# Values of the first attention: four of eight key tiles as three fp16 products

## The reference

```python
q = (v @ WQ).reshape(B, S, H, C)          # 16 batches, S = 1024, H = 8 heads, C = 64
k = (v @ WK).reshape(B, S, H, C)
val = (v @ WV).reshape(B, S, H, C)
scores = jnp.einsum('bshc,bthc->bsth', q, k) * SCALE
A = jax.nn.softmax(scores, axis=2)
u = jnp.einsum('bsth,bthc->bshc', A, val).reshape(B, S, H * C)
return u @ Wout + bout
```

## Time and profile before

| | us |
|---|---|
| median of 3 runs | 4938.34 (4937.33 to 4940.33) |
| the profiled execution | 4936.12 |
| its span | 4934.4 |
| TensorE busy in the span | 4631.5 (94%) |
| VectorE | 3639.3 (74%) |
| ScalarE | 3153.1 (64%) |
| GpSimd | 2212.3 (45%) |

### The profile page before, as it was taken

One profiled execution on the slowest core, in us unless ns is written; L12 is line 12 of the kernel. 1 busy time (PEld: TensorE's weight loads), 2 busy tenths in 40 slices (PEclk: granted clock), 3 DMA queues, 4 the chain that ended last, 5 costly groups with the idle time before them and its releaser, 6 DMA issues. The chain is left out here.

```text
span 4934.4 us, 105574 instructions
## 1 busy us (share of the span) xinstructions
PE 4631.5 (94%) x42323; PEld 2051.7 (42%) x42323; DVE 3639.3 (74%) x6356; ACT 3153.1 (64%) x3450; POOL 2212.3 (45%) x2149
## 2 busy tenths in 40 slices
PE   5999979999999999999999979999999999999965
PEld 3434423333333333333333334444444444444433
DVE  4666756666666666666666668888888888888878
ACT  2433426666666666666666638888888888888844
POOL 2233243333323232333333346666666666666656
PEclk9999989999999999999999979999999999999966
DMA  4211100000000000000000000000000000000001
GB/s 102 69 52 52 52 1 1 1 1 1 1 1 1 1 1 1 1 1 1 1 1 1 1 1 3 2 2 2 2 2 2 2 2 2 2 2 2 2 7 28
DMA packets 43620, 51.39 MB, mean 10 GB/s; under 512 B 33416, under 2 KB 33544, under 8 KB 43144
## 3 DMA queue, kind: packets, MB, share of 16 engines
q1 hardware_dynamic: 40440, 44.03, 3.3%
q10 hardware_dynamic: 2704, 0.72, 0.1%
HBM read 39.73 MB, written 4.19 MB: 9 GB/s over the span
## 5 line engine op out<-in xcount | busy, mean ns | idle before, releaser
L1686 DVE TENSOR_REDUCE a_mp<-psum 128x1 f32<-128x512 f32 x2072 | 1323.6, 685 | 668.1 <-PE psum L1563 654.4
L2412 DVE TENSOR_REDUCE f_mp<-psum 128x1 f32<-128x512 f32 (+2 forms) x2352 | 1471.5, 682 | 187.3 <-PE psum L2234 171.1
L1531 ACT ACTIVATE a_prob<-psum,escale 128x1024 f32<-128x1024 f32 x1024 | 1087.0, 1111 | 523.9 <-PE psum L1612 523.9
L2194 ACT ACTIVATE f_prob<-psum,escale_f 128x1024 f32<-128x1024 f32 x1152 | 1248.2, 1113 | 215.8 <-PE psum L2311 108.0
L1620 PE MATMUL psum<-a_prob,a_v 128*64 128x512 f32 x4104 | 993.7, 605 | 0.0
L2234 PE MATMUL psum<-f_kf,f_qf 64*128 64x512 f16 (+2 forms) x3658 | 651.6, 307 | 41.2 <-DVE f_mp L2412 32.1
L2048 POOL TENSOR_SCALAR f_hi<-f_raw,part 128x512 f16<-128x512 f32 x324 | 507.2, 1565 | 392.9 <-ACT f_raw L2152 386.6
L1451 POOL TENSOR_TENSOR a_u<-a_og,a_inv 128x512 f32<-128x512 f32 x129 | 134.5, 1042 | 1166.4 <-DVE a_inv L1701 1166.4
L2324 PE MATMUL psum<-f_prob,f_vh 128*32 128x512 f32 (+3 forms) x6144 | 614.7, 495 | 9.1 <-DVE f_oc L2434 7.3
L2303 PE MATMUL psum<-f_qf,f_kf 64*128 64x512 f16 (+3 forms) x3074 | 505.1, 327 | 18.6 <-ACT f_og L2157 18.2
L1620 PEld LDWEIGHTS psum<-a_prob,a_v 128*64 128x64 f32 x4104 | 248.8, 136 | 504.6 <-issue 501.0
(11 more groups left out here) (440 smaller groups left out, 6729.5 us busy)
## 6 DMA issues: line engine op xcount, KB each, us to landing
idx<-in_itok_BS_dram SPq DMA_DIRECT2D x36, 512.0 KB, 6.0
idx<-in_itok_BS_dram SPq DMA_DIRECT2D x54, 256.0 KB, 6.9
idx<-in_x_dram SPq DMA_DIRECT2D x18, 256.0 KB, 3.6
a_qh<-a_rowT SPq DMA_DIRECT2D x258, 1.0 KB
out_dram<-h SPq DMA_DIRECT2D x16, 256.0 KB, 2.6
f_qf<-f_rowT SPq DMA_DIRECT2D x130, 4.0 KB, 1.7
wd<-in_L_ffn_Wd_dram SPq DMA_DIRECT2D x2, 256.0 KB
bd<-in_L_ffn_bd_dram ACTq DMA_DIRECT2D x16, 2.0 KB
```

Of the source, the lines that this page charges most:

```text
L1531: act.activation(prob[:, part], k.psum[:, pair:pair + 2].rearrange("p b n -> p (b n)"), ACT.Exp, scale=k.escale[:]).then_inc(s.read, 1)
L1686: dve.tensor_reduce(mp[:, tg % 2, t + 4 * r, c:c + 1], bank_of(j + r), X, ALU.max)\
L2194: act.activation(prob[:, u % NPF], k.psum[:, pair:pair + 2], ACT.Exp, scale=k.escale_f[:])\
L2412: dve.tensor_reduce(side[:, at[0]:at[-1] + 1:step], bank_of(j + r)[:, 0:len(at) * width].rearrange("p (a b) -> p a b", b=width), X, ALU.ma ...
```

## The change

Key tiles 0, 1, 4 and 5 are multiplied by the values in three fp16 products instead of one fp32 product: low values x high exponentials, high values x low ones, high x high. For that the exponentials and the values are split into parts. Tiles 0 and 4 are split by GpSimd (`halve`: a cast, then a subtraction of 128x1024). Tiles 1 and 5 get their high part from a ScalarE copy, issued after the exponential of the following tile (2 or 6), and their low part from VectorE (`low`, in slots 3 and 7, after that slot's reductions). The exponential gets a bias of 6 ln 2, which the division by the sum takes out again. GpSimd also splits the values once a batch (`twice`, behind head 6's `add`).

The order is moved: the pairs are now (0,1), (2,3), (6,7), (4,5), in slots 4, 6, and 1 and 2 of the next head. (0,1) and (4,5) are the fp16 pairs. "out" moves from behind slot 3 to behind slot 5, the copy to `un` from behind tile 1 to behind tile 3, the inverse from slot 6 to slot 7. GpSimd's order in a head becomes: `halve` of tile 0, `split_q`, in head 4 `prepare_batch`, in head 5 `split_x`, `halve` of tile 4, `add`, in head 3 `squares`, in head 6 `twice`. Five more memsets are done before the stage's start. Four semaphores of an earlier stage are used again.

```diff
-A_PARTS = ((0, 1), (2, 3), (4, 5), (6, 7))
+A_PARTS = ((0, 1), (2, 3), (6, 7), (4, 5))
+A_PART_OF = {kt: p for p, part in enumerate(A_PARTS) for kt in part}
+A_HALVED = {0: 0, 1: 1, 4: 2, 5: 3}
+A_LEVEL = 6 * math.log(2.0)
-A_VALUES_AT = (2, 4, 6, 9)
+A_VALUES_AT = (4, 6, 9, 10)
-A_EXTRA = {0: (('x', 0),), 1: (('q', 2),), 3: (('out', -1),)}
-A_COPY_AT = 1
-A_INVERSE_AT = 6
+A_EXTRA = {0: (('x', 0),), 1: (('q', 2),), 5: (('out', -1),)}
+A_COPY_AT = 3
+A_INVERSE_AT = 7
...
+                def twice(b, par, n):
+                    here = v[:, par, :, 0]
+                    pool.tensor_copy(vh[:, par], here).then_inc(s.p, 1)
+                    passed(pool, k.seen, s.p, n + 5)
+                    pool.tensor_tensor(vl[:, par], here, vh[:, par], ALU.subtract).then_inc(s.p, 1)
+                def halve(G, kt, count):
+                    at = A_HALVED[kt]
+                    passed(pool, k.seen, s.read, count)
+                    pool.tensor_copy(ph[:, at], prob[:, kt]).then_inc(s.p_high, 1)
+                    passed(pool, k.seen, s.p_high, n_half(G, kt))
+                    pool.tensor_tensor(pl[:, at], prob[:, kt], ph[:, at], ALU.subtract).then_inc(s.p_low, 1)
...
+                pool.memset(ph[:], 0.0).then_inc(s.clear, 1)
+                pool.memset(pl[:], 0.0).then_inc(s.clear, 1)
+                pool.memset(vh[:, 1], 0.0).then_inc(s.clear, 1)
+                pool.memset(vl[:, 1], 0.0).then_inc(s.clear, 1)
+                pool.memset(level[:], A_LEVEL).then_inc(s.clear, 1)
...
+                        b = i * 2 + x // HEADS + 1
+                        halve(G, 0, n_stream(i, x, "exp", 0))
+                        split_q(G + 2, (x + 2) % 4, n_stream(i, x, "q", 0))
+                        if x % HEADS == 4:
+                            prepare_batch(b, (x // HEADS + 1) % 2, b * 6)
+                        if x % HEADS == 5:
+                            split_x(b, (x // HEADS + 1) % 2, n_stream(i, x, "x", 0))
+                        halve(G, 4, n_stream(i, x, "exp", 4))
+                        add(i * 2 + (x - 1) // HEADS, (x + 1) % 2, G + 1)
                         if x % HEADS == 3:
                             squares(i * 2 + x // HEADS)
+                        if x % HEADS == 6:
+                            twice(b, (x // HEADS + 1) % 2, b * 6)
...
                             act.activation(prob[:, part], k.psum[:, pair:pair + 2].rearrange("p b n -> p (b n)"),
-                                           ACT.Exp, scale=k.escale[:]).then_inc(s.read, 1)
+                                           ACT.Exp, scale=k.escale[:], bias=level[:]).then_inc(s.read, 1)
+                            if part in (2, 6):
+                                act.wait_ge(s.read, n_stream(i, x, "exp", part - 1))
+                                act.activation(ph[:, A_HALVED[part - 1]], prob[:, part - 1], ACT.Copy).then_inc(s.p_high_act, 1)
...
+                    if A_PARTS[p][0] in A_HALVED:
+                        pe.wait_ge(s.p_low, n_half(G, A_PARTS[p][0]))
+                        pe.wait_ge(s.p_low_dve, n_half(G, A_PARTS[p][1]))
+                        for kt in A_PARTS[p]:
+                            at = A_HALVED[kt]
+                            for a, b in ((vl, ph), (vh, pl), (vh, ph)):
+                                for half in range(2):
+                                    last = pe.matmul(ps[A_SUM][halves(half)], lhsT=a[:, bp, kt],
+                                                     rhs=b[:, at, half * HALF:(half + 1) * HALF],
+                                                     start=(kt == first and a is vl), stop=(kt == final and a is vh and b is ph),
+                                                     skip_group_check=True)
+                        last.then_inc(s.pv, 1)
+                        return
...
+                def low(G, kt):
+                    at = A_HALVED[kt]
+                    dve.wait_ge(s.p_high_act, n_half(G, kt))
+                    dve.tensor_tensor(pl[:, at], prob[:, kt], ph[:, at], ALU.subtract).then_inc(s.p_low_dve, 1)
...
                             for j, kind, of, part in ROUNDS[x][u]:
                                 read_out(i, x, j, kind, of, part)
+                            if u in (3, 7):
+                                low(i * AROUND + x, u - 2)
```

More of the change, by code:

```diff
@@ L1 @@
 from contextlib import ExitStack
+import math
 import numpy as np
@@ L702, in layer0 @@
         E = {name: k.sem("l0_" + name) for name in L_EVENTS}
+        k.spent, k.spent_at = [E[name] for name in ("gT", "eg", "wT", "gturn")], PAIRS_
         def first(pair):
@@ L1315, in attention1 @@
         prob = sb("a1_prob", [P, NPB, S], F32)
+        ph = sb("a1_ph", [P, 4, S], FP16)
+        pl = sb("a1_pl", [P, 4, S], FP16)
+        vh = sb("a1_vh", [P, 2, T, C], FP16)
+        vl = sb("a1_vl", [P, 2, T, C], FP16)
+        level = sb("a1_level", [P, 1], F32)
         un = sb("a1_un", [P, HALF], F32)
@@ L1336, in attention1 @@
         s.q_split = k.sem("a1_q_split")
+        s.p_high, s.p_high_act, s.p_low, s.p_low_dve = k.spent
         s.inverse = k.sem("a1_inverse")
@@ L1364, in n_pv, with n_half @@
             return NAV * (G + 1) + p + 1
+        def n_half(G, kt):
+            return k.spent_at + 2 * (G + 1) + kt // 4 + 1
         def bank_of(j):
@@ L1469, in _ @@
                 pool.memset(v[:, 1], 0.0).then_inc(s.clear, 1)
+                pool.memset(ph[:], 0.0).then_inc(s.clear, 1)
[3 more added lines that the diff above has]
+                pool.memset(level[:], A_LEVEL).then_inc(s.clear, 1)
                 pool.sem_inc(s.summed, 1)
                 pool.sem_inc(s.scaled, 2)
-                pool.wait_ge(s.clear, 6)
+                pool.sem_inc(s.p_high, 2)
+                pool.sem_inc(s.p_low, 2)
+                pool.wait_ge(s.clear, 11)
                 prepare_batch(0, 0, 0)
+                twice(0, 0, 0)
                 split_x(0, 0, 1)
@@ L1515, in copy_out @@
                     act.activation(un[:], ps[A_SUM], ACT.Copy).then_inc(s.copied, 1)
+                act.sem_inc(s.p_high_act, 2)
                 for n, (kind, of, part) in enumerate(A_START_STREAM):
@@ L1519, in _ @@
                     read_out(0, -1, kind, of + 1, 2 * (n % 2))
-                act.wait_ge(s.clear, 6)
+                act.wait_ge(s.clear, 11)
                 for i in range(NB // 2):
@@ L1529, in _ @@
                                 continue
-                            act.wait_ge(s.pv, n_pv(G - 1, part // 2))
+                            act.wait_ge(s.pv, n_pv(G - 1, A_PART_OF[part]))
                             act.activation(prob[:, part], k.psum[:, pair:pair + 2].rearrange("p b n -> p (b n)"),
-                                           ACT.Exp, scale=k.escale[:]).then_inc(s.read, 1)
+                                           ACT.Exp, scale=k.escale[:], bias=level[:]).then_inc(s.read, 1)
+                            if part in (2, 6):
+                                act.wait_ge(s.read, n_stream(i, x, "exp", part - 1))
+                                act.activation(ph[:, A_HALVED[part - 1]], prob[:, part - 1], ACT.Copy).then_inc(s.p_high_act, 1)
                             if part == A_COPY_AT:
@@ L1613, in score, with values @@
                     return last
-                def values(x, p):
+                def values(G, x, p):
                     bp = (x // HEADS) % 2
+                    first, final = A_PARTS[0][0], A_PARTS[-1][-1]
+                    if A_PARTS[p][0] in A_HALVED:
[11 more added lines that the diff above has]
+                        return
                     for kt in A_PARTS[p]:
@@ L1621, in values @@
                                              rhs=prob[:, kt, half * HALF:(half + 1) * HALF],
-                                             start=(kt == 0), stop=(kt == T - 1), skip_group_check=True)
+                                             start=(kt == first), stop=(kt == final), skip_group_check=True)
                     last.then_inc(s.pv, 1)
@@ L1629, in _ @@
                 last.then_inc(s.pv, NAV - sum(at >= T for at in A_VALUES_AT))
-                pe.wait_ge(s.clear, 6)
+                pe.wait_ge(s.clear, 11)
                 for n, (kind, of, part) in enumerate(A_START_STREAM):
@@ L1654, in _ @@
                                             pe.wait_ge(s.read, n_stream(i, x, "exp", A_PARTS[p][-1]))
-                                            values(x, p)
+                                            values(G, x, p)
                                         if at == u + T:
                                             pe.wait_ge(s.read, n_stream(i, x - 1, "exp", A_PARTS[p][-1]))
-                                            values(x - 1, p)
+                                            values(G - 1, x - 1, p)
                                 else:
@@ L1669, in _ @@
                         pe.wait_ge(s.read, SS + SR * (NB // 2))
-                        values(-1, p)
+                        values(NB * HEADS - 1, -1, p)
```

(1 more changed line is left out.)

## The result

The changed kernel takes 5524.7 us (5522.7 to 5530.4), the kernel before 4938.2 in the same set of runs: 1.119 times as long (95% interval 1.1173 to 1.1206), +586 us where 462 were forecast. The direction and the place were right; the time lies 35 us above the top of the range.

What follows compares the result with a forecast made beforehand. TensorE, the bound before, would wait on equal loops through VectorE and GpSimd: 157.2 us a batch against 132.8, x16 = +390; clock 64, start 6, end 2 make +462, 5400 us on the median. Range 5190 to 5490.

Steps and rivals of the forecast that it cites:

- The saving of TensorE: In the values matmuls, two of four pairs becoming fp16 save 0.48 us each, 0.95 a head.
- the reading of "out": Before tile 7's score matmul, TensorE waits 0.21 us a head until "out" has been read.
- the start: Before the stage, GpSimd's extra clearing of buffers takes 4 to 9 us, taken as 6, all exposed.
- rival (e): `low` is ready before the first fp16 values matmul, so TensorE stays the bound: 4824 us; chance 3%.
- VectorE's loop: The first fp16 values matmul waits for `low`, queued behind VectorE's reductions: 17.85 us a head undisturbed.
- GpSimd's loop: `add` waits for the inverses; `halve` and `split_q` follow, and slot 4's maxima wait for that split: 17.8 us a head.
- The blocking: `low` waits out GpSimd's q subtraction because two-input VectorE instructions contend with it: 18.55 us a head instead of 17.8.
- 3.3 us for that head: In head 5, `low` asks in the middle of `split_x`'s 2.13 us subtraction, delaying the first fp16 values matmul by 3.3.
- the clock: In heads 4 and 7, long TensorE idling halves the clock, 2 us lost each: +64 us, bounds 0 and 200.
- my 6.30: TensorE's way from the first fp16 values matmul of a head to slot 7's maxima: 6.3 us.
- the end: After the last head, a second values matmul and its parts add 2 us.
- Rival (d): GpSimd's cast of tile 4 gets ahead of `low`, values matmul at 19.6 us: up to 5500; chance 9%.

Runs made afterwards that it cites:

- the two kernels without parts: Changed kernel with no exponential parts made and no waits for them: 4954.2 us; the same with all four pairs in fp32: 5057.5 us.
- opening them singly: Changed kernel with GpSimd's `add` behind the next head's `split_q`: 5426.0 us; separately, with tile 1's copy and `low` made earlier (slot 1): 5477.0 us.
- together: Changed kernel with both edits, `add` behind the next head's `split_q` and tile 1's copy and `low` made earlier: 4956.6 us.
- with it taken away: Changed kernel with VectorE's two-input subtraction in `low` replaced by a one-input reduction of the same tile: 5425.8 us.
- the fillers: Changed kernel with extra matmuls of constants into the free sum bank where TensorE waits: 5315.4 us.
- the kernel with the order mended: Against the all-fp32 kernel without parts in the moved order (5057.5 us): maxima before V(4,5) in slot 2, before the score tile in slot 6: 4964.8 us.

## Why the prediction was right in kind and wrong in size

- The saving of TensorE, 0.95 a head: measured 0.81 (the two kernels without parts). Nearly right, and 119 us of moved order and start, of which the prediction had 33 (27 for the reading of "out", 6 for the start), undo it. In the changed kernel the waits at the banks lie under the longer waits for `split_q` and `low` (1.59 and 0.78 in head 6), so this didn't spoil the sum. It did spoil rival (e): even with every part ready in time the kernel would have been 16 us slower than before, not 114 faster.
- VectorE's loop and GpSimd's loop, equally long: right, shown by opening them singly (99 and 48 us) and together (568). `low` cost 1.22 (I took 1.25).
- The blocking: right; 99 us with it taken away, 0.75 x 128 = 96 by the prediction. In head 5 it went the other way round. VectorE's `low` was issued just ahead of GpSimd's subtraction:
```profile
2210.69 1.22 DVE L1765 TENSOR_TENSOR a_pl<-a_prob,a_ph 128x1024 f16<-128x1024 f32 x1
2210.71 3.19 POOL L1469 TENSOR_TENSOR a_xl<-a_xraw,a_xh 128x1024 f16<-128x1024 f32 x1 [0.18 <-POOL a_xh L1467]
```
  so GpSimd was blocked (3.19 for 2.13) and TensorE hardly. I had 3.3 us for that head and it is 1.3 (V(0,1) from 2188.63 to 2212.05 is 23.4 us; less 18.5 and 3.7 of clock): 32 us less in all.
- **The step that failed is the clock**: the prediction lets it fall only in heads 4 and 7 ("2 us lost: x2 heads x16 = +64", with bounds of 0 and 200). That it falls and costs time on the path was right; the term was mis-sized. It measured 209. The same windows as the earlier trace rows, for the plain head 6 above:
```profile
2062.00:2064.00 2.00, 1.22 (x10) 0.70 (x12) 2.00 (x3) 0.15 (x1) 1.89 (x1) 0.95 0.00 0
2064.00:2066.00 2.00, 2.00 (x14) 0.81 (x9) 0.40 (x2) 0.00 (x0) 1.93 (x1) 0.50 0.01 4
2066.00:2068.00 2.00, 2.00 (x24) 1.52 (x20) 1.29 (x2) 0.45 (x1) 0.19 (x1) 0.69 0.01 1
```
  Before the fall TensorE had idled 1.59 us, done one M and idled 0.78; the clock fell to 1.2 GHz when it was already at work on V again. I had taken the one row with an unbroken idle of 5.50 as the kind of wait that matters. Seven of eight heads fall (only head 5, with 0.33 and 1.64 idle, doesn't in the batch I read). From V(0,1) to M(7), my 6.30, it is 6.34 in head 5 and 7.91 in head 6 (2063.14 to 2071.05), and 10.0 in head 4: (6 x 1.6 + 3.7) x 16 = 213, beside the 209 of the fillers. Head 7 takes 10.3 instead of 7.8 in about every second batch; over all 128 heads this way is 224 us longer than 128 x 6.34.
- The start: M and V begin 9.6 us later (734.6 and 744.2), I had 6; the end, +2, is within 1.

In sum: 390 + 64 + 8 was forecast. Of the 586, 209 are the clock, some 10 the start, and the 367 that are left the loops, with the blocking and the savings in them. So the miss of 124 is 145 of clock and 4 of start too little, and some 25 of loops and end too much, where head 5's 32 lie.

Rival (d) is given as "up to 5500", but its own V at 19.6 makes 1.05 x 128 = 134 more, 5534. That this is near the measured 5525 is chance: in (d) GpSimd's cast of tile 4 gets ahead of `low`, and the rows of head 6 show `low` ahead of the cast.

## What to carry to other kernels

Before moving work to engines with room, draw the loop: which instruction of theirs starts after what of the bound engine, what is queued ahead of it, and where the bound engine stands until it is done. Two loops of the same length hide each other: removing either one gave 99 and 48 us, removing both gave 568, the clock's loss included, since either loop alone kept TensorE waiting enough to lower the clock (0.93 and 0.92 over the run). When a full TensorE begins to wait in each round, price its clock in each round, not only behind the longest waits.

## What the runs showed of the hardware that I had not expected

- The clock can fall to 1.2 GHz after two waits of 1.6 and 0.8 us with a pair of matmuls between them (0.50 in the window 2064 to 2066), and matmuls of constants in these waits kept it at 1.00 in the loop.
- An exponential of 128x1024 from PSUM with a scale and a bias per partition took 1.204 us in the mean, with the scale alone 1.111. The Trainium skill (ScalarE: Activation LUTs, What ACT_TABLE_LOAD costs) has each per-partition operand at about 93 ns; the trace agrees with 93. I had priced the bias at nothing. What it costs in time was not tried apart; the kernel with the order mended has the bias and is 27 us slower than before, some 10 of them the start; how much of the other 17 is the bias is open.
- GpSimd's clearing of 128x4096 fp16 took 3.51 us, that of 128x2048 fp32 1.80, and that of 128x4096 fp32, in the run with the order mended, 3.51 again: by elements, not by bytes.
